# Six-index records for SyncE, and the last layer norm as two scalar-tensor operations on VectorE

## The reference, cut to what matters

```python
# layer 0: an expert MLP, sequence by sequence
h = gelu(x @ Wi[e0] + bi[e0])                 # 256 -> 1024
r = h @ Wo[e0] + bo[e0] + x                   # 1024 -> 256
z = (r - mean) * rsqrt(var + 1e-12)
x = z * gamma[e0] + beta[e0]
# layer 1: an adapter with a small expert matrix
a = gelu(x @ down_W.T + down_b)               # 256 -> 64
a = a @ expert_W[e1].T + expert_b[e1] + domain_emb[e1]
u = a @ up_W.T + up_b + x
out = (u - mean) * rsqrt(var + 1e-5) * ln_gamma + ln_beta
```

## Time and profile before

| | |
|---|---|
| time, median of 3 runs | 537.85 us (537.72 to 538.39) |
| the profiled execution | 537.86 us, its span 535.9 us |
| PE busy / weight loads | 493.2 us (92%) / 432.0 us (81%) |
| VectorE busy | 423.7 us (79%) |
| ScalarE busy | 381.8 us (71%) |
| GpSimd busy | 315.0 us (59%) |
| granted TensorE clock | 0.983 of full speed |
| shares of the chain of waits | SyncE's queue 37%, PE 35%, nothing that shows 11%, VectorE 6% |
| ScalarE's `x_hi` waited for `x_T` | 72.4 us in 47 waits |

### The profile page before, as it was taken

The page is one execution under the profiler, slowest core; times in us unless marked ns, Lnnn a source line. Parts: engine busy times, 40 slices in busy tenths (PEclk is TensorE's granted clock), DMA queues, the critical chain, the costliest instruction groups (busy, mean ns, idle before and its releaser), DMA issues.

```text
span 535.9 us, 19427 instructions
## 1 busy us (share of the span) xinstructions
PE 493.2 (92%) x5778; PEld 432.0 (81%) x5779; DVE 423.7 (79%) x935; ACT 381.8 (71%) x1099; POOL 315.0 (59%) x521
## 2 busy tenths in 40 slices
PE   5699999999999999999989999999999999999962
PEld 3489988888888878888878888888878888888951
DVE  6677888888888888788888888887888877677762
ACT  2688777787877777777778777787777876677741
POOL 5043666666656566565665566655666655555554
PEclk9799999999999999999999999999999999999995
DMA  4734333333333333323333333333333222222111
GB/s 115 245 95 103 87 91 94 79 91 89 93 93 80 87 92 89 92 78 90 91 90 91 84 91 87 90 90 87 87 88 89 63 64 58 61 62 56 46 32 29
DMA packets 70256, 45.83 MB, mean 86 GB/s; under 512 B 43969, under 2 KB 61778, under 8 KB 70098
## 3 DMA queue, kind: packets, MB, share of 16 engines
q1 hardware_dynamic: 69200, 45.25, 31.5%
q10 hardware_dynamic: 1026, 0.21, 0.2%
HBM read 36.51 MB, written 8.91 MB: 85 GB/s over the span
## 4 chain that ended last, share of the span: by engine, by line
SPq 37%; PE 35%; issue 11%; DVE 6%; POOL 4%; DMA 3%; ACT 2%; POOLq 1%; DVEq 0%; ACTq 0%
SPq L258 9%; SPq L322 8%; SPq L372 7%; SPq L330 7%; PE p_h L918 5%; PE p_h L919 4%; PE p_h L920 4%; PE p_o L928 4%; PE p_o L926 4%; PE p_o L927 4%; SPq L338 3%; PE p_d L937 2%; DMA x_T<-in_xT 2%; POOL rs L484 2%; PE p_t L959 2%
## 5 line engine op out<-in xcount | busy, mean ns | idle before, releaser
L918 PE MATMUL p_h<-x_hi,W 128*128 128x128 f16 x1088 | 194.0, 220 | 5.6 <-issue 5.3
L919 PE MATMUL p_h<-x_lo,W 128*128 128x128 f16 x1088 | 193.4, 220 | 0.0
L920 PE MATMUL p_h<-x_hi,W 128*128 128x128 f16 x1088 | 193.3, 220 | 0.0
L484 POOL TENSOR_TENSOR rs<-mv,neg_half 128x2 f32<-128x2 f32 (+1 forms) x70 | 67.6, 966 | 162.4 <-DVE mv L797 156.8
L581 ACT ACTIVATE h<-p_h,bi_tile 128x128 f32<-128x128 f32 x544 | 152.6, 362 | 0.4 <-PE p_h L920 0.4
L926 PE MATMUL p_o<-W,h_hi 128*128 x544 | 148.3, 273 | 0.0
L927 PE MATMUL p_o<-W,h_hi 128*128 x544 | 148.3, 273 | 0.0
L928 PE MATMUL p_o<-W,h_lo 128*128 x544 | 148.3, 273 | 0.0
L764 DVE SCALAR_TENSOR_TENSOR h_lo<-h,h_hi 128x512 f16<-128x512 f32 x136 | 124.5, 915 | 1.0 <-ACT h_hi L589 0.9
L918 PEld LDWEIGHTS p_h<-x_hi,W 128*128 x1088 | 106.7, 98 | 19.7 <-issue 18.3
L919 PEld LDWEIGHTS p_h<-x_lo,W 128*128 x1088 | 106.7, 98 | 1.5
(11 more groups left out here) (153 smaller groups left out, 715.7 us busy)
## 6 DMA issues: line engine op xcount, KB each, us to landing
stage<-in_w SPq DMA_DIRECT2D x56, 256.0 KB, 2.6
x_nat<-in_x SPq DMA_DIRECT2D x136, 64.0 KB, 2.1
out<-y SPq DMA_DIRECT2D x136, 64.0 KB, 2.0
x_T<-in_xT SPq DMA_DIRECT2D x134, 64.0 KB, 2.2
W<-in_w SPq DMA_DIRECT2D x8, 256.0 KB, 4.1
g_t<-in_gamma SPq DMA_DIRECT2D x1, 1024.0 KB, 7.7
W<-in_expert_W SPq DMA_DIRECT2D x2, 128.0 KB, 3.0
upT<-in_up_W SPq DMA_DIRECT2D x2, 64.0 KB, 2.6
```

The lines of the kernel that those rows point to most:

```text
L484: pool.tensor_tensor(rs[:, both], mv[:, both, 1], neg_half[:, both], ALU.pow).then_inc(rs_done, 1)
L918: mm(p_h[parity][:, c, :], hi, x_hi[:, parity, k, :], start=(k == 0), stop=False)
L919: mm(p_h[parity][:, c, :], hi, x_lo[:, parity, k, :], start=False, stop=False)
L920: ins = mm(p_h[parity][:, c, :], lo, x_hi[:, parity, k, :], start=False, stop=(k == KD - 1))
```

## The change

- SyncE reads one record of six integers in each step: two for the rows of tile i, two for `x_T` of tile i+2, two for the result of tile i-5 (`IDX_SP`). The sorting writes them in that layout, in three pieces, the first of which lets ScalarE start its first transfer. The load of two indices behind `y_done` is gone.
- The first chunk of an expert's weights is one index, loaded once for eight steps; a chunk's address is that register plus a constant. SyncE's loop body has 8 steps in place of 4. The list of 64 chunk numbers becomes one of 8. At the start all eight first chunks hang on one load in place of two loads of four.
- `y` is made by two scalar-tensor operations on VectorE: (yg - mean) * lng, in place, between `mv` (L797 before) and the second half of `h_lo`; and times `rs` plus `lnb`, where L812 stood. L466 and L468 on GpSimd are gone, and `y_done` comes from VectorE.
- GpSimd's multiplication into `yg` also waits until VectorE has made the first half of `h_lo` of the step before.

```diff
-IDX_SRC, IDX_DST = 0, SLOTS
-IDX_EXP = 2 * SLOTS + 3
+IDX_SP = 0
+IDX_PE = IDX_SP + 6 * STEPS
+IDX_EXP = IDX_PE + 4 * STEPS + 3
...
             def load_later(j, slot_n):
+            def load_later(j, expert, m, slot_n):
                 if not isinstance(j, int) or j >= SLOTS_W:
                     sp.wait_ge(w_lo, j - (SLOTS_W - 1))
-                c = index(sp, IDX_CHUNK + FIRST_CHUNKS + j, CHUNKS - 1)
-                sp.dma_start(stage[:, slot_n, :], t["w"][bass.ds(c * P, P), :]).then_inc(w_in[slot_n], 16)
+                sp.dma_start(stage[:, slot_n, :], t["w"][bass.ds((expert + m) * P, P), :]).then_inc(w_in[slot_n], 16)
...
                 if weights:
-                    load_later(i + AHEAD, weights[2])
-
-                if exists(i):
-                    b = indices(sp, 2 * i + IDX_SRC, 6 if exists(i + 2) else 2, B - 1)
+                    if weights[0] == 0:
+                        expert[0] = first_chunk(weights[1])
+                    load_later(i + AHEAD, expert[0], weights[0], weights[2])
+                if exists(i + 2) or exists(i - 5):
+                    b = indices(sp, 6 * i + IDX_SP, 6, SLOTS - 1)
                 if exists(i + 2):
-                    load_turned(b[4:6], i + 2, parity)
+                    load_turned(inside(b[2:4]), i + 2, parity)
                 if exists(i - 5):
                     sp.wait_ge(y_done, i - 4)
-                    to = indices(sp, 2 * i + (IDX_DST - 10), 2, SLOTS - 1)
...
-            run(sp, step, SLOTS_W, AHEAD)
+            run(sp, step, NCH, AHEAD)
...
-                if exists(i - 5):
-
-                    last = y[:, 1 - parity, :]
-                    pool.wait_ge(z2_done, i - 4)
-                    if isinstance(i, int) and i == 5:
-                        pool.wait_ge(ln_in, 2 * 16)
-                    pool.tensor_tensor(last, last, lng[:, :], ALU.mult).then_inc(zg_done, 1)
-                    pool.wait_ge(zg_done, i - 4)
-                    pool.tensor_tensor(last, last, lnb[:, :], ALU.add).then_inc(y_done, 1)
                 if exists(i - 3):
...
                     pool.wait_ge(z1_done, i - 2)
+
+                    pool.wait_ge(hlo_half, 2 * min(i, TILES) - 1 if isinstance(i, int) else 2 * i - 1)
+
+                    need(pool, y_done, i - 4)
                     pool.tensor_tensor(yg[:, 1 - parity, :], z1[:, :], g_t[:, bass.ds(e_third * D, D)], ALU.mult)\
                         .then_inc(yg_done, 1)
...
-            v.tensor_copy(idx[:, IDX_SRC:IDX_DST], p_t[0:1, 0:SLOTS]).then_inc(idx_ready, 1)
+            sp_idx = idx[:, IDX_SP:IDX_PE].rearrange("a (t r) -> a t r", r=6)
+            src = p_t[0:1, 0:SLOTS].rearrange("a (t n) -> a t n", n=2)
+            v.tensor_copy(sp_idx[:, 0:TILES, 0:2], src).then_inc(idx_ready, 1)
+            v.tensor_copy(sp_idx[:, 0:TILES - 2, 2:4], src[:, 2:TILES, :]).then_inc(idx_ready, 1)
...
                 if exists(i - 4):
                     v.bn_aggr(mv[:, 1, :], st2[:, :]).then_inc(mv2_done, 1)
+                if exists(i - 4):
...
+                    dve.wait_ge(mv2_done, i - 3)
+                    v.scalar_tensor_tensor(yg[:, parity, :], yg[:, parity, :], mv[:, 1, 0:1], lng[:, :],
+                                           ALU.subtract, ALU.mult).then_inc(t2_done, 1)
                 if exists(i - 1):
                     split_h(i - 1, 1 - parity, 1)
...
                 if exists(i - 4):
 
+                    dve.wait_ge(t2_done, i - 3)
                     dve.wait_ge(rs_done, i - 1)
...
-                    v.tensor_scalar(y[:, parity, :], yg[:, parity, :], mv[:, 1, 0:1], rs[:, 1:2],
-                                    ALU.subtract, ALU.mult).then_inc(z2_done, 1)
+                    v.scalar_tensor_tensor(y[:, parity, :], yg[:, parity, :], rs[:, 1:2], lnb[:, :],
+                                           ALU.mult, ALU.add).then_inc(y_done, 1)
```

More of the change, by code:

```diff
@@ L316, in _, with inside @@
                 sp.dma_start(downb[half, :], t["down_b"].rearrange("(p a) -> p a", a=1)).then_inc(adapter_in, 16)
+            def inside(b):
+                return [nc.s_assert_within(r, 0, B - 1, skip_runtime_bounds_check_because="the sorting clips every index")
+                        for r in b]
             def load_turned(b, i, parity):
@@ L331, in load_natural, with first_chunk @@
                       .then_inc(xnat_in[parity], 16)
-            def load_later(j, slot_n):
+            def load_later(j, expert, m, slot_n):
                 if not isinstance(j, int) or j >= SLOTS_W:
                     sp.wait_ge(w_lo, j - (SLOTS_W - 1))
-                c = index(sp, IDX_CHUNK + FIRST_CHUNKS + j, CHUNKS - 1)
-                sp.dma_start(stage[:, slot_n, :], t["w"][bass.ds(c * P, P), :]).then_inc(w_in[slot_n], 16)
+                sp.dma_start(stage[:, slot_n, :], t["w"][bass.ds((expert + m) * P, P), :]).then_inc(w_in[slot_n], 16)
+            def first_chunk(place_n):
+                return index(sp, IDX_CHUNK + place_n, CHUNKS - NCH)
             sp.wait_ge(idx_ready, CHUNK_READY)
[L342 to L348, removed]
+            expert = first_chunk(0)
+            for m in FIRST_ORDER:
+                sp.dma_start(first_stage[m], t["w"][bass.ds((expert + m) * P, P), :]).then_inc(first_in[m], 16)
             sp.wait_ge(idx_ready, SRC_READY)
-            b = [indices(sp, 2 * i + IDX_SRC, 2, B - 1) for i in range(2)]
-            load_turned(b[1], 1, 1)
+            load_turned(indices(sp, IDX_SP + 6, 2, B - 1), 1, 1)
+            expert = [first_chunk(1)]
             for j in range(AHEAD):
-                load_later(j, j % SLOTS_W)
+                load_later(j, expert[0], j, j % SLOTS_W)
             sp.dma_start(g_t[:, :], t["gamma"].partition_broadcast(P)).then_inc(g_in, 16)
@@ L539, in _ @@
             nc.scalar.copy(b_s[:, :], ph_flat[0][:, 0:D]).then_inc(b_ready, 1)
-            act.wait_ge(idx_ready, SRC_READY)
-            b = indices(act, IDX_SRC, 2, B - 1)
+            act.wait_ge(idx_ready, FIRST_READY)
+            b = indices(act, IDX_SP, 2, B - 1)
             for n in range(2):
@@ L682, in _ @@
             link(v.tensor_reduce(ord_f[:, :], cube[0:1, :, :], AX.X, ALU.add))
[L683 to L684 removed]
+            v.tensor_scalar(idx[:, IDX_CHUNK:IDX_LEN], ord_f[:, :], float(NCH), None, ALU.mult).then_inc(idx_ready, 1)
             link(v.tensor_tensor(cube[:, :, :], ahead[:, :, :], rows(two_pairs[:, :], E0), ALU.mult))
@@ L756, in _ @@
             link(v.scalar_tensor_tensor(row, row, float(B), empty, ALU.add, ALU.mult))
-            v.tensor_tensor(idx[:, IDX_DST:2 * SLOTS], row, p_u[0:1, 2 * SLOTS:3 * SLOTS], ALU.add)\
+            v.tensor_tensor(sp_idx[:, 5:TILES + 5, 4:6], row.rearrange("a (t n) -> a t n", n=2),
+                            p_u[0:1, 2 * SLOTS:3 * SLOTS].rearrange("a (t n) -> a t n", n=2), ALU.add)\
                 .then_inc(idx_ready, 1)
@@ L797, in step @@
                     v.bn_aggr(mv[:, 1, :], st2[:, :]).then_inc(mv2_done, 1)
+                if exists(i - 4):
+                    if isinstance(i, int) and i == 4:
+                        dve.wait_ge(ln_in, 2 * 16)
+                    dve.wait_ge(mv2_done, i - 3)
+                    v.scalar_tensor_tensor(yg[:, parity, :], yg[:, parity, :], mv[:, 1, 0:1], lng[:, :],
+                                           ALU.subtract, ALU.mult).then_inc(t2_done, 1)
                 if exists(i - 1):
```

15 lines of the change are left out of this document (6 added, 9 removed).

## The result

The changed kernel takes 519.05 us (median; 518.74 to 519.06) beside 538.06 us of the kernel before on the same chip: a ratio of 0.9645, with a 95% interval of 0.9626 to 0.9664. One further execution of it was disturbed (1429 us) and is left out of the comparison. The forecast was 523.5 us, with a range from 519.0 to 547.5. The direction and the bound came out; the gain was 19.0 us where 14.4 were forecast. The forecast was made from 537.85 us; against that the ratio gives 518.8 us, just under the lower end of the range. The profiled execution took 518.74 us, 516.9 of them its span; that of before took 537.86.

The account below looks back on a forecast made before the run. SyncE's queue was taken as the bound from 138 to 433 us, elsewhere PE with a ring through VectorE and GpSimd. Terms of -11.0, -1.0, -2.1 and -0.3 sum to -14.4, from 537.86 to 523.5 us; range 519 to 547.5.

Parts of the forecast that it names:

- The bound: SyncE's queue limits the tiles from 138 to 433 us; without that, a tile takes 7.10 us.
- SyncE's loads: Fewer index loads cut SyncE's step from 7.41 to 6.41 us; the forty tiles gain 11.0 us.
- `y` off GpSimd: Two fewer GpSimd operations free up to 1.1 us of VectorE per tile, counted as 0.
- The first half of `y`: New VectorE operation between `mv` and `h_lo` takes about 0.41 us in idle time, counted as 0.
- What it does to `rs`: `rs` on GpSimd follows the new VectorE operation; bounded by -6.6 and +22 us, taken as -1.0 us.
- The bound from below: `rs` lets `h_lo` go at once, so `z` starts up to 0.1 us sooner per tile, -6.6 us.
- The first rival: Second half of `h_lo` waits out `rs`, 0.33 us more per tile, 547 us in all; chance 0.29.
- The end: After the last sums, `y` is finished sooner and needs no index load before its transfer: -2.1 us.
- The start: One more small VectorE copy in the sorting, against earlier first `x_T` loads: -0.3 us.
- The second and the third rival: `rs` keeps its turn partly, 530 to 537 us, chance 0.10; or records do little, 534 us, chance 0.06.
- the sign by which the prediction called itself wrong: Tiles behind 433 us, which SyncE doesn't bound, change their time.

Follow-up runs that it names:

- The records alone: Changed kernel with the output's normalisation made as before, one operation of VectorE and two of GpSimd: 525.34 us, ratio 0.9764.
- the kernel with both moves and the old records: Changed kernel with second-half `h_lo` ahead of `a1s`, `t2` behind `z`, and SyncE's records, start loads and order of before: 533.37 us, ratio 0.9924.
- the output's norm alone: Kernel before with the output's normalisation in two operations of VectorE and none of GpSimd, SyncE untouched: 534.73 us, ratio 0.9950.

## Why the prediction was right about the bound, and the step where it was wrong

*The bound.* Right. It was read from the slack: SyncE's queue from 138 us on, and 7.10 us for a tile without it. The records alone give 7.097, and the kernel with both moves and the old records gives 7.375, the old number, whatever VectorE does.

*SyncE's loads, -11.0 us.* Right in size: 40 x (7.376 - 7.097) = 11.2, with some luck in the choice of the four tiles. The slack of 0.69 us stated there was also right: one load of 0.47 us put back fits in nearly free, a second one is paid by 0.45 us a tile.

*`y` off GpSimd, 0.* Right as far as it was reasoned: `W` and `h_lo` are 0.53 us shorter each, and giving half of that back changes nothing. But with `t2` behind `z`, where `z` gains only 0.01 us, the kernel is still 0.3, 0.5 and 0.5 us better than with the records alone in the three stretches between the transposes (ahead of the 15th tile, the forty, behind). These 1.4 us had no term in the prediction, and their cause stays open.

*The first half of `y`, 0.* Nearly right: it fits, but it takes 0.48 us and not 0.41. `x_lo`, of the same form and size, takes 0.41 in the rows above and was a poor stand-in.

*What it does to `rs`, -1.0 us.* This is the step that failed, by its size. The bound from below was the truth: `h_lo` isn't held at all. I took 0.015 us a tile; `z` came 0.06 us sooner on the mean of the forty tiles (0.05 in three tiles of four, 0.08 in the fourth, where `rs` isn't held either). The most that it could give I had reckoned at 0.1 us, with the new operation ending 0.65 us behind the start of `mv`; it ends 0.71 behind. In the 67 tiles between the first and the last transposes 0.057 us each make 3.8 us in place of 1.0, and the tiles gained by about as much as `z`: 0.05 us a tile between the kernels that differ only in `t2`'s place. So the one to one of the prediction holds here; the step to the second transpose takes 0.17 us with the records alone and in the changed kernel alike. Measured from the records alone, the tiles gained 2.4 us (the forty), 0.9 behind them and 0.8 ahead, about 4.1 us in all, of which 2.8 belong to `t2`'s place; the rest is what had no term. (The other 0.6 ahead of the 15th tile came with the records, 98.57 to 97.94 us, and I had given them nothing there.) Having set bounds of -6.6 and +22, I chose a value next to nothing of the lower one and called it near. With the 1.4 us that had no term, the 0.6 of the records and the early start, that put the result just under the range.

*The first rival, 0.29.* Wrong on the premise that `rs` is like the operations of the earlier trace rows. `h_lo` takes 0.69 us beside it. The argument that I gave against it, that a column costs 0.14 us and so the time is in the power, fits: 64 columns take 10.75 us, and `h_lo` passes beside them. The rule of the Trainium skill, SBUF — State Buffer, "SBUF: two separate sides", of a lock kept for the whole instruction, holds here for `yg`, whose 256 columns make `h_lo` 1.21 us long, and doesn't hold for `rs`; the measurement decides.

*The end, -2.1 us.* 1.82 measured. *The start, -0.3 us.* 1.23 in the profiled pair, most of which goes with the low clock, as the two groups of profiles show.

*The second and the third rival.* Neither happened; the third is ruled out by the records alone. But the sign by which the prediction called itself wrong did come: the 13 tiles behind 433 us, which SyncE doesn't bound, went from 89.08 to 88.02 us, 0.08 a tile. It contradicted the prediction's own `rs` term, which shortens every tile.

The sum of what the profiled pair gained more than forecast: 2.5 us in the forty tiles, 1.5 ahead of them and 1.1 behind, together 5.1, less the 1.0 that I had spread over them; 0.9 at the start; -0.3 at the end. That makes 4.7, and 523.5 - 4.7 = 518.8, beside 518.74 measured.

## What to carry to other kernels

Find the queue that waits for nobody, and price its loads of registers as instructions: where its step is a little longer than that of the next ring, putting the numbers of a step into one record is worth the difference, here 11.2 us over 40 tiles; what the step gains beyond that is only slack. Then look at the short operation on which the ring turns (here `rs`) and at what the other engine has beside it: an instruction with two inputs that starts ahead of it made it 0.23 us longer, and moving two such away from it brought 9.6 us. Moving only one of them left the other to hold it up in most tiles (3.4 us slower with the one moved, 3.1 faster with the other). When two bounds are 0.3 us apart, do both edits before judging either: the output's norm alone was worth 3.0 us, and 6.3 where the records were in place.

## What the runs showed of the hardware that was not expected

- GpSimd's power costs by the column: 0.56 us for one, 0.69 for two, 10.75 for 64, so some 0.16 us each. An operation of VectorE with two inputs that starts behind it passes beside it (0.69 to 0.78 us in place of 0.68). One that started 0.1 us or more ahead of it holds it up (0.93 to 0.97 us in place of 0.69); one that started 0.04 us ahead didn't.
- A transpose that has had to wait for its input makes the next one late too, by a fixed 0.06 us: the step to the second takes 0.17 us whether the first came 0.1 us late (changed kernel) or 0.4 us (kernel before), and 0.11 where it wasn't late.
- SyncE's load of a record of six numbers takes 0.73 us in one step and 1.28 in the next, by turns, and that of two 0.46 to 0.50. Records are 24 bytes apart, so if the row begins at a multiple of 16 bytes, every second one does; the kernel before, whose steps are 8 bytes apart, alternates in the same way (0.73 and 1.26). That this is the reason wasn't tried.
- In the first 30 us PE's low clock falls earlier in some executions than in others, in kernels with the old loads and with the new; the first transposes came at 38.44 to 39.89 us, so a comparison of two profiles can have up to 1.4 us in it from this.
